# Eight steps of the first expert pass run between the stages of the last sequences of a language-model layer

## The reference, cut to what matters

```python
h = concat(fine[ids], softmax(cluster[ids] + b) @ coarse)           # embedding: gather, small softmax
x = layernorm(h)
y = x + memory(rms_norm(x))      # decayed linear attention over the 512 tokens of a sequence
h = h + y + op(gelu(rms_norm(y) @ read_mix + bias))
x = layernorm(h)                 # 4096 tokens
shared = mean over 2 shared experts of (silu(x @ g) * (x @ u)) @ d
p, e   = top6(softmax(x @ router.T + bias))                          # 64 experts, F = 64
slot   = running count of tokens of expert e, in token order; kept while slot < 768
out    = h + shared + sum over 6 of p * expert_e(x)                  # each expert: gate, up, down
```

## Time and profile before

| | us |
|---|---|
| median of 3 runs | 579.55 (574.35 to 579.94) |
| the profiled execution | 577.37 |
| its span, from first to last instruction | 575.6 |
| mean granted TensorE clock | 0.857 |

### The profile page before, as it was taken

How to read it: one execution, slowest core, us unless ns; L and a number is a source line. 1 busy time by engine, 2 the same in 40 slices (tenths; PEclk the granted TensorE clock), 3 DMA queues, 4 the chain that set the end, 5 groups by cost and what they waited for, 6 DMA issues and landing times.

```text
span 575.6 us, 11744 instructions
## 1 busy us (share of the span) xinstructions
PE 417.2 (72%) x2715; PEld 350.3 (61%) x2715; DVE 443.9 (77%) x1686; ACT 281.0 (49%) x806; POOL 404.7 (70%) x426
## 2 busy tenths in 40 slices
PE   2577877748674626879999999999999999960000
PEld 2456655536553425779999988899888887640000
DVE  2677999999989764998888669888999887486222
ACT  2125455244253305557777777777776564410000
POOL 7770037777777777777777777777777777777773
PEclk9999878868777556999999999999999898995555
DMA  7999201111114212778888899999988885253221
GB/s 181 258 247 215 37 20 51 51 51 52 51 51 124 92 50 92 217 211 245 244 242 237 240 250 245 253 265 251 255 234 252 240 224 152 68 138 85 60 64 41
DMA packets 128296, 91.13 MB, mean 158 GB/s; under 512 B 15224, under 2 KB 118245, under 8 KB 127974
## 3 DMA queue, kind: packets, MB, share of 16 engines
q1 hardware_dynamic: 64230, 38.63, 25.9%
q0 software_dynamic: 13312, 26.59, 16.1%
q10 hardware_dynamic: 50688, 25.17, 14.6%
HBM read 46.99 MB, written 44.04 MB: 158 GB/s over the span
## 4 chain that ended last, share of the span: by engine, by line
POOL 33%; DVE 27%; PE 20%; issue 13%; DMA 3%; ACT 3%; POOLq 0%; ACTq 0%; DVEq 0%
POOL shared L1104 31%; PE bank L455 5%; PE bank L444 4%; PE bank L435 3%; PE bank L344 3%; DMA emb<-table_dram,idx 2%; POOL emb L1073 1%; DVE struck L814 1%; DVE hid L1019 1%; DVE emb L757 1%; DVE x L775 1%; DVE shared L740 1%; PE bank L394 1%; DVE top_place L847 1%; DVE top_place L911 1%
## 5 line engine op out<-in xcount | busy, mean ns | idle before, releaser
L1089 POOL DMA_INDIRECT x_rows<-x,to_row x192 | 189.3, 986 | 94.4 <-issue 58.2
L1104 POOL DMA_INDIRECT shared<-o_rows,to_got x192 | 182.6, 951 | 58.5 <-issue 58.5
L455 PE MATMUL bank<-w_down,hid 64*128 x768 | 111.8, 286 | 10.9 <-DVE hid L1019 9.4
L623 ACT ACTIVATE w_now<-w_in 128x128 f32 x384 | 87.4, 298 | 61.2 <-issue 30.6
L455 PEld LDWEIGHTS bank<-w_down,hid 64*128 64x128 f32 x768 | 93.4, 189 | 23.9 <-issue 14.8
L444 PE MATMUL bank<-x_t,w_now 128*128 128x128 f32 x768 | 104.3, 280 | 0.1
L444 PEld LDWEIGHTS bank<-x_t,w_now 128*128 128x128 f32 x768 | 95.8, 196 | 0.6 <-ACT x_t L626 0.5
L939 DVE SCALAR_TENSOR_TENSOR emb<-shared,gate_of,emb 128x128 f32<-128x128 f32 x192 | 67.0, 351 | 36.7 <-DMA shared<-o_rows,to_got 31.6
L1019 DVE TENSOR_TENSOR hid<-hid,bank 64x512 f32<-64x512 f32 x96 | 66.2, 690 | 33.5 <-ACT hid L631 30.9
L1025 DVE COPY lanes<-bank 128x512 f32<-128x512 f32 x96 | 66.4, 691 | 3.6 <-PE bank L455 0.7
L631 ACT ACTIVATE hid<-bank 64x512 f32<-64x512 f32 x96 | 56.5, 589 | 19.6 <-PE bank L444 18.0
(11 more groups left out here) (210 smaller groups left out, 601.3 us busy)
## 6 DMA issues: line engine op xcount, KB each, us to landing
lanes<-x_rows SPq DMA_DIRECT2D x384, 64.0 KB
o_rows<-lanes ACTq DMA_DIRECT2D x96, 256.0 KB
x_rows<-hid_s SPq DMA_DIRECT2D x2, 2048.0 KB, 18.9
x_rows<-x,to_row POOLq DMA_INDIRECT x192, 2.2
shared<-o_rows,to_got POOLq DMA_INDIRECT x192
w_in<-gate_t_dram SPq DMA_DIRECT2D x1, 2048.0 KB, 23.0
w_in<-up_t_dram SPq DMA_DIRECT2D x1, 2048.0 KB, 32.8
w_down<-down_t_dram SPq DMA_DIRECT2D x2, 1024.0 KB, 17.6
```

The lines of the kernel that those rows point to most:

```text
L455: last = pe.matmul(bank_d[k][:, c * P:c * P + P], hid[k][:, c * P:c * P + P], w[:, bass.ds(at[c], P)], start=(c == 0), stop=(c == GROUP - ...
L623: last = act.activation(w_now[k][:, c, :], w[:, bass.ds(at[c], P)], ACT.Copy)
L1089: pool.indirect_dma_start(x_rows, bass.IndirectOffsetOnAxis(ap=to_row[b][:, t * 8 + j:t * 8 + j + 1], axis=0), x3[b][:, t, :], None, bound ...
L1104: pool.indirect_dma_start(got[n % G_RING][:, j, :], None, o_rows[p], bass.IndirectOffsetOnAxis(ap=to_got[b][:, t * 8 + j:t * 8 + j + 1], a ...
```

## The change

What it does, by parts:

- The steps 0 to 7 are written into the front. `STEP_AT` gives each a tick, and `front` writes `step(eng, q)` when it comes, on TensorE, ScalarE (`act_step`) and VectorE. The steps from 8 on follow the front as before. The waits for the passes' tables move into the steps (`tile_w` of the step's own pass).
- The steps' PSUM banks are others, and steps 0 and 1 wait until the front is done with the bank they take (`h`, `state`, `x2`, `z`, `scores` and `h2` of all eight sequences).
- The tick tables are new and finer. Sequence 0 has one of its own, sequence 1 begins at tick 153 and each later one 500 after the one before it.
- SP waits for the embedding rows of sequences 0 and 1 before it issues the zeros and the weights.
- `dve_fetch` starts at step 8 and not 1, the gates are spread 10, 12, 10 over the passes, and the sums are planned from step 39 and not 43.

The ticks of sequence `b` from 1 on are `153 + 500 * (b - 1)` plus the table's.

```diff
-FETCH_STEP, STEPS_PER_TOKENS = 43.0, 2.9
-
-GATES_IN = (16, 6, 10)
-
-
-
-SPACING = 80
-DVE_AT = dict(logits=0, exp_sum=37, h=98, var1=109, newton1=148, xn=154, xn_dec=181, y_dec=238, x1=239,
-              scores=245, state=247, x2=263, ms2=293, newton2=305, xn2=309, hx=337, h2=366, var3=378,
-              newton3=392, x3=397, rl=414, top=422, norm=425, gates=427, rows=428, cols=432, tabs=486)
-PE_AT = dict(exp_t=0, coarse=9, xn_t=155, y=166, zs=175, state=213, mem=233, xn2_t=279, vals=303, op=321,
-              x3_t=369, router=380, pos=396, count=407, tile=419)
-ACT_AT = dict(cluster_exp=1, exp_t=36, rs1=134, xn_t=168, y=221, z=229, squares=251, rs2=280, xn2_t=313,
-              gelu=325, rs3=385, x3_t=399, router_exp=400)
-LAST_TICK = 487
+FETCH_STEP, STEPS_PER_TOKENS = 39.0, 2.9
+
+GATES_IN = (10, 12, 10)
+
+
+
+
+SPACING, SECOND = 500, 153
+DVE_AT = (dict(logits=0, exp_sum=55, h=70, var1=143, newton1=266, xn=325, x1=1035, y_dec=1106,
+               xn_dec=1121, scores=1177, state=1369, x2=1567, ms2=1691, newton2=1741, xn2=1758, hx=1835,
+               h2=2158, var3=2210, newton3=2285, x3=2336, rl=2502, top=2510, norm=2526, gates=2530,
+               rows=2534),
+          dict(logits=0, exp_sum=410, h=858, var1=985, newton1=1220, xn=1275, xn_dec=1463, y_dec=1770,
+               scores=1807, state=1853, x1=1884, x2=1976, ms2=2053, newton2=2082, xn2=2124, hx=2314,
+               h2=2498, var3=2564, newton3=2645, x3=2668, rl=2917, top=2977, norm=3104, gates=3196,
+               rows=3202, cols=3205, tabs=3345))
+PE_AT = (dict(exp_t=226, coarse=505, xn_t=828, y=1050, zs=1203, state=1305, mem=1558, xn2_t=1957,
+               vals=2020, op=2190, x3_t=2426, router=2459, pos=2556),
+          dict(exp_t=533, coarse=688, xn_t=1513, y=1624, zs=1771, state=1842, mem=1936, xn2_t=2276,
+               vals=2391, op=2569, x3_t=2800, router=2935, pos=3172, count=3308, tile=3422))
+ACT_AT = (dict(cluster_exp=76, exp_t=172, rs1=215, xn_t=881, y=1184, z=1204, squares=1696, rs2=1856,
+               xn2_t=2022, gelu=2032, rs3=2355, x3_t=2488, router_exp=2539),
+          dict(cluster_exp=293, exp_t=542, rs1=1272, xn_t=1502, y=1678, z=1797, squares=2020, rs2=2082,
+               xn2_t=2351, gelu=2467, rs3=2698, x3_t=2882, router_exp=2990))
+STEP_AT = (4339, 5388, 5891, 6041, 6101, 6294, 6356, 6565)
+LAST_TICK = 6575
...
-        bank_x, bank_g, bank_h, bank_d = banks[0:2], banks[2:4], banks[4:6], banks[6:8]
+        bank_x, bank_g, bank_d, bank_h = (bank_e, bank_a0), (bank_a1, bank_b0), (bank_b1, bank_c0), (bank_c1, bank_p)
...
-        def front(eng, one):
-
-            for tick in range((BATCHES - 1) * SPACING + LAST_TICK):
+        def begins(b):
+            return SECOND + (b - 1) * SPACING if b else 0
+
+        def front(eng, one, step):
+
+            for tick in range(LAST_TICK + 1):
                 for b in range(BATCHES):
-                    if 0 <= tick - b * SPACING < LAST_TICK:
-                        one(eng, b, tick - b * SPACING)
+                    if tick >= begins(b):
+                        one(eng, b, tick - begins(b))
+                for q, at in enumerate(STEP_AT):
+                    if at == tick:
+                        step(eng, q)
...
-        FETCH_AT = {1 + b: b for b in range(BATCHES)}
+        FETCH_AT = {len(STEP_AT) + b: b for b in range(BATCHES)}
-            first, steps = (2, STEPS_OF[p] - 2) if p == 0 else (STEP0[p], STEPS_OF[p])
+            first, steps = (len(STEP_AT) + 1, STEPS_OF[p] - len(STEP_AT) - 1) if p == 0 else (STEP0[p], STEPS_OF[p])
...
+
+            for b in range(2):
+                sp.wait_ge(sem(f"gathered{b}"), 16 * TILES)
             sp.wait_ge(sem("set"), 1)
...
         def pe_x_t(pe, q):
             k = q % 2
+            if q < 2:
+
+                pe.wait_ge(sem(("h", "state")[q]), BATCHES)
...
         def pe_in(pe, q):
             k = q % 2
+            if q == 0:
+                pe.wait_ge(sem("x2"), BATCHES)
+            if q == 1:
+                pe.wait_ge(sem("z"), 2 * BATCHES)
+                pe.wait_ge(sem("scores"), BATCHES)
...
         def pe_down(pe, q):
             k = q % 2
+            if q in STEP0:
+                pe.wait_ge(sem("tile_w"), STEP0.index(q) + 1)
             at = tile_weights(mybir.EngineType.PE, q)
+            if q == 0:
+                pe.wait_ge(sem("z"), 2 * BATCHES)
+                pe.wait_ge(sem("scores"), BATCHES)
+            if q == 1:
+                pe.wait_ge(sem("h2"), BATCHES)
...
                 pe.wait_ge(sem("hid"), STEPS)
+
+                pe.wait_ge(sem("x3_t"), BATCHES)
+                pe.wait_ge(sem("tile_w"), len(PASSES))
+                pe.wait_ge(sem("kept"), 3 * BATCHES)
...
-            front(pe, one)
-
-            pe.wait_ge(sem("tile_w"), len(PASSES))
-            pe.wait_ge(sem("kept"), 3 * BATCHES)
-            pe.wait_ge(sem("weights"), 16 * 7)
-            for q in range(STEPS + 2):
+            def step(pe, q):
+                if q == 0:
+                    pe.wait_ge(sem("weights"), 16 * 7)
                 if q < STEPS:
                     pe_x_t(pe, q)
                 if 0 <= q - 1 < STEPS:
                     pe_in(pe, q - 1)
                 if q >= 2:
                     pe_down(pe, q - 2)
+
+            front(pe, one, step)
+            for q in range(len(STEP_AT), STEPS + 2):
+                step(pe, q)
...
+        def act_step(act, q):
+            w = w_in[:, :, :].rearrange("d e f -> d (e f)")
+            if q == 0:
+                act.wait_ge(sem("weights"), 16 * 7)
+            if q < STEPS:
+                k = q % 2
+                if q in STEP0:
+                    act.wait_ge(sem("tile_w"), STEP0.index(q) + 1)
+                at = tile_weights(mybir.EngineType.Activation, q)
+                wait(act, "pe_in", q - 1)
+                for c in range(GROUP):
+                    last = act.activation(w_now[k][:, c, :], w[:, bass.ds(at[c], P)], ACT.Copy)
+                last.then_inc(sem("w_now"), 1)
+                act.wait_ge(sem("pe_x_t"), q + 1)
+                act.activation(x_t[k][:, :], bank_x[k][:, :], ACT.Copy).then_inc(sem("x_t"), 1)
+            if q >= 1:
+                k = (q - 1) % 2
+                act.wait_ge(sem("pe_in"), q)
+                wait(act, "pe_down", q - 2)
+                act.activation(hid[k][:, :], bank_g[k][0:F, :], ACT.Silu).then_inc(sem("silu"), 1)
+            if q >= STORE_LAG:
+                act_store(act, q - STORE_LAG)
...
+            front(act, act_front, act_step)
+            for q in range(len(STEP_AT), STEPS + 1):
+                act_step(act, q)
...
-            front(dve, one)
-            for q in range(STEPS + 2):
+            def step(dve, q):
...
+            front(dve, one, step)
+            for q in range(len(STEP_AT), STEPS + 2):
+                step(dve, q)
```

More of the change, by code:

```diff
@@ L315, in pe_front @@
         def pe_front(pe, b, r):
-            if r == PE_AT["exp_t"]:
+            at = PE_AT[min(b, 1)]
+            if r == at["exp_t"]:
                 pe.wait_ge(sem("cluster_exp"), b + 1)
@@ L408, in pe_front @@
                           skip_group_check=True).then_inc(sem("pe_pos"), 1)
-            if r == PE_AT["count"] and last_of_pass(b):
+            if last_of_pass(b) and r == at["count"]:
                 pe.wait_ge(sem("part_count"), b + 2)
@@ L413, in pe_front @@
                           skip_group_check=True).then_inc(sem("pe_count"), 1)
-            if r == PE_AT["tile"] and last_of_pass(b):
+            if last_of_pass(b) and r == at["tile"]:
                 pe.wait_ge(sem("tile_e"), PASS_OF[b] + 1)
@@ L510, in one @@
             def one(pe, b, r):
-                if b == 0 and r == PE_AT["xn_t"]:
+                if b == 0 and r == PE_AT[0]["xn_t"]:
                     pe.wait_ge(sem("prep2"), 1)
@@ L658, in dve_front @@
         def dve_front(dve, b, r):
+            at = DVE_AT[min(b, 1)]
             e = emb[b]
-            if r == DVE_AT["logits"]:
+            if r == at["logits"]:
                 wait(dve, "pe_exp_t", b)
@@ L669, in dve_front @@
                    .then_inc(sem("cluster_logits"), 1)
-            if r == DVE_AT["exp_sum"]:
+            if r == at["exp_sum"]:
                 dve.wait_ge(sem("cluster_exp"), b + 1)
@@ L701, in dve_front @@
                 last.then_inc(sem("xn"), 1)
-            if r == DVE_AT["xn_dec"]:
+            if r == at["xn_dec"]:
                 wait(dve, "pe_state", b)
@@ L787, in dve_front @@
                    .then_inc(sem("router_logits"), 1)
-            if r == DVE_AT["top"]:
+            if r == at["top"]:
                 wait(dve, "pe_pos", b)
                 dve_top(dve, b)
-            if r == DVE_AT["norm"]:
+            if r == at["norm"]:
                 dve_norm(dve, b)
-            if r == DVE_AT["gates"]:
+            if r == at["gates"]:
                 dve_kept(dve, b)
-            if r == DVE_AT["rows"]:
+            if r == at["rows"]:
                 dve_rows(dve, b)
```

(10 more changed lines are left out.)

110 lines of the change are left out of this document (45 added, 65 removed).

## The result

| us | before | changed |
|---|---|---|
| median | 577.22 (574.35 to 579.94, 4 runs) | 585.08 (584.17 to 590.27, 4 runs) |
| the profiled execution | 577.37 | 585.33 |
| its span | 575.6 | 583.6 |
| mean granted TensorE clock | 0.857 | 0.853 |

The ratio of the medians is 1.0159 (95% interval 1.0116 to 1.0203): slower by 1.6%. For the profiled execution 585 was forecast (+7.5; it came to +8.0), with a POOL wait of 14.6 us in the middle of the sends as the cause.

What follows compares the result with a forecast made beforehand. POOL's string of sends and gathers was taken as the bound. Head gain -7.1 plus gap +14.6 made +7.5 on the profiled 577.37, so 585 us, with the steps hidden; range 575 to 597.

Steps and rivals of the forecast that it cites:

- The bound: POOL's string of 192 sends and 192 gathers sets the time; TensorE and VectorE do not.
- The gap: POOL waits before send 73 for `to_row` 3, held up by step 0 in ScalarE's order: +14.6 us.
- the ring: `to_row` 3 waits for send 72's landing through SP, TensorE, ScalarE and VectorE; send 73 waits for `to_row` 3.
- The head: Sequence 0 up to the first send: -6.8 landing, +1.9 stall, -2.2 order; sum -7.1 us, first send at 73.1.
- The stall on sequence 2: VectorE's `logits` of sequence 2 waits for rows landing late beside the zeros: 0 to +3.3 us, taken as +1.9.
- The steps in the front: Steps 2 to 7 in sequence 7's tail, mostly in TensorE's idle time: +4 us, step 8 begins at 252.
- Pass 0: Its stores are ready at 333.3, its gathers can begin at 335.5: steps just hidden.
- Pass 1: Ready at 421.3 against gathers at 425.7: hidden, or +6 us if none of the added gates overlaps.
- The clock: After the standstill TensorE would run slow, at 1.2 GHz, putting the front's tail nearer the late case than +4 us.
- the late case: Rival, chance 0.16: front's tail with steps costs 10 or more, POOL waits for pass 0 or 1 stores: 590 to 598.
- No gap: Rival, chance 0.11: `to_row` 3 is written before send 72 ends, only the head's -7.1 is left: 570.
- Cancelling: Rival, chance 0.29: head gain near 12 and gap near 12.5 cancel, about 578, within 572 to 583.

Runs made afterwards that it cites:

- The square of four: Kernel before, SP's two waits alone (575.15 us), changed kernel without them (586.7), changed kernel (585.08); first sends 80.17, 78.39, 75.40, 70.5 to 75.2.
- the kernel with step 0 late: Changed kernel with step 0 at tick 5380, just before step 1, not 4339: 571.86 us, ratio 0.9906 to the kernel before.

## Why the prediction was right, and where its sizes were off

**The bound** held: all 8.0 us are accounted for in POOL's string alone, and on the chips at usual speed each experiment's span follows from its first send and POOL's later waits to about 2 us. That the sum, +7.5, came within 0.5 us is luck: the gap was 2.7 too long and the head's gain 1.2 too small, and against these 3.9 stood 2.4 of wait in pass 1, 1.7 of slower sends and 0.4 in the rest, none of them forecast.

**The gap** was there, at the send that was named and by the ring that was named. From the start of send 72 to that of send 73 it is 13.1 us (164.97 to 178.09), forecast 15.8. TensorE stood from 138.2 to 171.5, forecast 135 to 173. Term by term: SP's first load came 3.0 us after send 72's start (167.96) where I took 4.9; the fourth load's issue and landing took 3.5 (to 171.51), forecast 1.6 + 1.9; the transposes 1.1, where I took 1.97; from the copy of `x_t` to the start of the last instruction of `rows` 4.5 (172.63 to 177.11), forecast 0.58 + 0.45 + 0.5 + 1.03 + 2.05 = 4.6 to its end; then 0.8 to POOL's start after that end, forecast 0.85. So two terms were too long, by 2.8 together, and most of that was misread rows. The 4.9 was counted from 171.45, the start of send 71; from send 72, at 172.72, it is 3.6. And the 1.97 in the earlier trace rows is x8, the transposes of steps 0 and 1; one step has four, so half of that, and they took 1.09 here, at a granted clock of 0.50. With both rows read rightly the forecast gap is 12.3, against 11.85. The 0.65 us left in the first term stays open.

**The head** came to -8.3 against -7.1. Its parts were off in both directions. The landing of sequence 0 was right (9.64, 10.0 forecast), and so was the order behind `x2` (39.78 to the send 32.1, before 34.7: -2.6, forecast -2.2). The stall on sequence 2 was 4.45 where I took 1.9 and allowed 3.3: the rows landed at 27.4, 9 us after the end of their last gather's issue, while the zeros were being written. And from `logits` 0 to `x2` I took nothing; without its stall that way takes 39.78 - 9.64 - 4.45 = 25.7 us, against 28.6 before, -2.9. The split between the two parts of the change was wrong in my mind: I gave the waits 6.8, less 1.9 for the stall, and the tables 2.2. The square of four gives 1.8 and 4.8, within the spread of single profiles. The agreement of the sum is no better than that spread: the same head sent first anywhere from 70.53 to 75.18. In the old order an early landing of sequence 0 buys little, since its path passes through the other sequences' late rows.

**The steps in the front** cost what I took: TensorE went on at 172.39 and came to step 8 at 251, 78.6 us, forecast 77.2. ScalarE loaded three activation tables more (22 in all, 19 before, 1.28 us each), four were forecast.

**Pass 0** was forecast ready at 333.3 and POOL at 335.5. From the kernels in which POOL did wait there, the first gather starts some 3.7 us after the last store's issue (326.27 to 329.99, 331.16 to 334.91). By that, the store at 329.47 was good for 333.2, and POOL came at 333.25. So the steps came out hidden with no room at all, where I had counted on 2 us.

**Pass 1** was forecast hidden, or +6 if none of its gates overlap. It was a wait of 2.67 us, the term that failed. I carried over 88.0 us from step 33 to 67; it was 92.2. In pass 1, from about 385 on, the stores come in groups some 3.56, 2.48 and 2.14 us apart, 8.17 for three steps where plain ones take 7.70. Of the 34 intervals between these stores ten hold both a gate tile and part of a sum and take 3.36 to 3.57; none of the others, with one of the two or neither, takes more than 2.57. So where the two fall together a step is 1 us longer, and the next two give only half of it back, whatever VectorE's idle sum over the stretch says. In the kernel before five intervals hold both, and two of them are long; why not all five is open. And store to gather was 4.5 us, not 2.2.

**The sends** were taken as unchanged and came 9 ns slower each, +1.7 us in 192. The change is not the cause: the seven other kernels with the new tables, on chips at usual speed, have 981 to 988 ns, and the old tables with SP's waits 992.

**The clock.** In the standstill the granted clock was 0.55, the lower level for most of it. Behind it the first 5 us, to 176, still ran at 0.50, with step 0's transposes and the first `zs` matmuls (L365, 3.62 us); from 180 to 205 it was 1.00. Over the 34 us it was 0.91, TensorE being busy 23.8 of them with the work that had piled up. From 205 to 222, where TensorE was busy 9.5 of 17 us, it was down to 0.58 again. I had expected dense work only at the very end of the front. The Trainium skill ("TensorE: Matmul & The Clock Gate", Part 1) says that an idle array falls to the lower clock and that sustained activity brings the full one back; the trace agrees in both. It spoke for a tail nearer the late case only because I had applied it to a stretch that I took to be thin; that inference failed. The same 190 to 222 that stood at 0.50 before was at 0.78.

**The rivals.** No gap would have been 570, and the kernel with step 0 late shows that figure to be sound: 571.86. Cancelling needed a head near 12 and a gap near 12.5; the gap was there (11.85, nearer than my 14.6), the head was 8.3. The late case is what one gets when the gap alone is mended: the first gather waited 11.16 us, and the time was 582, below that case's 590 to 598.

## What to carry to other kernels

When an instruction that depends on a DMA's round trip is merged into the order of another chain, look in each engine's list at what stands behind it, and follow that to the engine that feeds the DMA: a ring that closes there costs the whole round trip, here 12 us, and moving that one instruction to where its rows are long there gives it back. Work that is done early is worth only what the next fixed point in the order lets through; here eight early steps were stopped at the first sum. Where two losses lie side by side, mending one shows the other and not the gain, so mend the common cause.

## What the runs showed of the hardware that was not expected

The same head gave first sends from 70.53 to 75.18 in five profiles, though nothing in it differs. In the two latest, 73.34 and 75.18, VectorE waits 1.5 us for TensorE at `x2` of sequence 0, in the others 0.7 at most. The granted clocks don't separate them (20 to 42 us: 0.77 in the one at 71.87, 1.00 in the other four), and the cause stays open. It is larger than several of the terms above, so a single profile of the head can't settle 2 us.

A gather of 128 rows issued while the zeros go out lands 9 us later instead of about 2 (sequence 2's last, issued from 17.13 to 18.08, landed at 27.4; sequence 0's last, issued before the zeros, is used at 9.64). Holding the zeros back by one sequence more moved the late landing on to the next sequence (3.70 and 2.83 us at sequence 3 in two kernels, in place of 4.45 at sequence 2). From a store's issue to the start of the gather that waited for it, it was 3.6 to 3.8 us at the end of the sends (three kernels) and 4.4 to 4.9 in the middle of the gathers (seven kernels).

And on one chip five kernels, the one before among them, took 1.58 times as long, with stretches in which only POOL went on as ever; the cause is open.
